# Attention: the fourth head group's causal mask moved from TensorE to GpSimd, and its value product moved behind two more units of row maxima

## What is computed

```python
q, k, v = sh(xn @ Wq.T + bq), sh(xn @ Wk.T + bk), sh(xn @ Wv.T + bv)   # 16 heads of 8
scores = (einsum('bhqd,bhkd->bhqk', q, k) + rel_shift(rel)) * 8 ** (-0.5)
scores = where(mask, NEG, scores)                                      # causal: key after query
p = softmax(scores, axis=-1)
ctx = einsum('bhqk,bhkd->bhqd', p, v)
return ctx @ Wo.T + bo
```

## Time and profile before

| | |
|---|---|
| median of 3 runs | 6254.8 us |
| profiled execution, its own time | 6261.56 us |
| its span | 6259.8 us |
| TensorE busy with matmuls | 5663.6 us (90%) |
| VectorE busy | 4182.8 us (67%) |
| ScalarE busy | 2815.0 us (45%) |
| GpSimd busy | 2135.9 us (34%) |
| exponentials L468 | 640, mean 1451 ns |
| selects L306 and L307 | 480 each, means 645 and 644 ns |
| reductions L362 | 1920, mean 686 ns |

### The profile page before, as it was taken

How to read it: one execution, slowest core, us unless ns; L and a number is a source line. 1 busy time by engine, 2 the same in 40 slices (tenths; PEclk the granted TensorE clock), 3 DMA queues, 4 the chain that set the end, 5 groups by cost and what they waited for, 6 DMA issues and landing times. The chain is left out here.

```text
span 6259.8 us, 121332 instructions
## 1 busy us (share of the span) xinstructions
PE 5663.6 (90%) x38029; PEld 3508.3 (56%) x38029; DVE 4182.8 (67%) x9572; ACT 2815.0 (45%) x4608; POOL 2135.9 (34%) x3000
## 2 busy tenths in 40 slices
PE   7997999999997899879997999889988989886677
PEld 5664444444443677457754776467754556634464
DVE  6875666666665788358854886378835656578764
ACT  4553222222222455535553555445554645533344
POOL 5661000000000666146632665166610012253312
PEclk9998999999998999989998999999998999987799
DMA  4332222222223656046622564066600000000002
GB/s 133 103 106 98 97 96 98 95 96 98 99 94 89 165 155 160 9 121 158 157 63 68 155 160 116 7 165 157 157 13 5 0 7 0 1 4 0 0 2 62
DMA packets 526329, 527.02 MB, mean 84 GB/s; under 512 B 55699, under 2 KB 436706, under 8 KB 503781
## 3 DMA queue, kind: packets, MB, share of 16 engines
q1 hardware_dynamic: 517684, 517.90, 29.7%
q10 hardware_dynamic: 8320, 5.25, 0.4%
HBM read 337.88 MB, written 185.07 MB: 84 GB/s over the span
## 5 line engine op out<-in xcount | busy, mean ns | idle before, releaser
L362 DVE TENSOR_REDUCE a_mx<-a_unit 128x2 f32<-128x512 f32 (+1 forms) x1920 | 1288.2, 686 | 411.8 <-PE a_unit L564 405.5
L468 ACT ACTIVATE a_prob<-a_slot 128x1536 f32<-128x1536 f32 x640 | 928.5, 1451 | 643.3 <-PE a_slot L587 503.4
L562 PE MATMUL a_unit<-a_sk,a_sq 96*128 96x256 bf16 (+3 forms) x5120 | 746.0, 250 | 75.8 <-DMA a_sk<-a_kscratch 41.2
L1177 ACT ACTIVATE f_silu<-f_pG 128x512 f32<-128x512 f32 x528 | 314.8, 598 | 935.0 <-PE f_pG L1252 921.0
L564 PE MATMUL a_unit<-a_maskq,identb 128*128 128x256 bf16 (+1 forms) x1920 | 602.1, 314 | 0.0
L1119 DVE TENSOR_TENSOR f_gated<-f_spread,f_silu 128x512 f32<-128x512 f32 x512 | 354.5, 692 | 351.1 <-ACT f_silu L1177 307.0
L1229 PE MATMUL f_pO<-f_hidden,f_wd 128*128 128x512 f32 x1056 | 545.7, 598 | 13.8 <-DVE f_hidden L1121 13.3
L1252 PE MATMUL f_pG<-f_xnT,f_wg 128*128 128x512 f32 x1056 | 541.1, 594 | 0.0
L1256 PE MATMUL f_pU<-f_xnT,f_wu 128*128 128x512 f32 x1056 | 540.2, 593 | 0.0
L562 PEld LDWEIGHTS a_unit<-a_sk,a_sq 96*128 96x128 bf16 (+1 forms) x5120 | 384.2, 99 | 277.2 <-DVE a_mx L362 154.2
L306 POOL TENSOR_SCALAR_AFFINE_SELECT a_prob<-a_prob 128x512 f32<-128x512 f32 x480 | 309.5, 645 | 578.0 <-ACT a_prob L468 561.4
(11 more groups left out here) (409 smaller groups left out, 11173.0 us busy)
## 6 DMA issues: line engine op xcount, KB each, us to landing
f_spread<-f_scratch SPq DMA_DIRECT2D x1024, 128.0 KB, 2.9
a_sq<-a_qscratch SPq DMA_DIRECT2D x128, 768.0 KB, 5.8
a_sk<-a_kscratch SPq DMA_DIRECT2D x160, 384.0 KB, 6.6
a_qscratch<-a_parts SPq DMA_DIRECT2D x288, 192.0 KB, 2.3
a_qscratch<-a_parts SPq DMA_DIRECT2D x288, 128.0 KB, 2.2
a_kscratch<-a_parts SPq DMA_DIRECT2D x160, 192.0 KB, 2.4
a_kscratch<-a_parts SPq DMA_DIRECT2D x160, 128.0 KB, 2.2
a_qscratch<-a_parts SPq DMA_DIRECT2D x288, 64.0 KB, 1.8
```

The lines of the kernel that those rows point to most:

```text
L362: v.tensor_reduce(dst, src, op=ALU.max, axis=AX.X, negate=True).then_inc(red_done, 1)
L468: act.activation(prob[gr % 2][:, :], slot[:, :], ACT.Exp, scale=SCALE).then_inc(exp_done, 1)
L562: pe.matmul(bank[:, at * wide:(at + 1) * wide], q, sk[b][0:KM, gr * GH + h, 0:wide], start=(at == 0), stop=False)
L1177: act.activation(silu[c % 2][:, :], pG[c % 2][:, :], ACT.Silu).then_inc(silu_done, 1)
```

## The change

GpSimd's `causal` is called for group 3 as well, between the first subtraction and the second BF16 copy of the parts. SELECTED becomes 4, so `scores` writes no mask matmul for any group (L584 and L591 are gone) and `values` waits for the selects in all groups. The value product of group 3, which is done a step late, goes from behind maxima(0) to behind maxima(2). The extra `if` and `sem_inc` around the call only split the block in two.

```diff
@@ -330,6 +330,10 @@
                         pt = parts[j % 2]
                         g.sem_inc(apart, 1)
                         chain.link(g.tensor_tensor(rest[:, :, :], f32s[:, :, :], pt[:, :, 0, :], op=ALU.subtract))
+                    causal(3)
+                    if is_seq(n + 4):
+                        pt = parts[j % 2]
+                        g.sem_inc(apart, 1)
                         chain.link(g.tensor_copy(pt[:, :, 1, :], rest[:, :, :]))
                         g.tensor_tensor(pt[:, :, 2, :], rest[:, :, :], pt[:, :, 1, :], op=ALU.subtract
                                         ).then_inc(parts_done, 1)
@@ -624,9 +628,9 @@
                             ins = pe.transpose(ring[1][:, t * P:(t + 1) * P], xn[:, t, :], ident)
                         ins.then_inc(t_pe, 1)
                     maxima(0)
-                    values(n - 1, (j + 1) % 2, 3)
                     maxima(1)
                     maxima(2)
+                    values(n - 1, (j + 1) % 2, 3)
                     if is_seq(n + 4):
                         if once(n, -4):
                             pe.wait_ge(w_qk, W_QK)
@@ -2637,7 +2641,7 @@
         step(n // 2, n % 2)
 
 
-SELECTED = 3
+SELECTED = 4
```

## The result

| | before | after |
|---|---|---|
| median of the runs | 6258.3 us (4 runs, 6252.84 to 6265.35) | 6362.74 us (4 runs, 6355.85 to 6367.54) |
| profiled execution, its own time | 6261.56 us | 6365.27 us |
| its span | 6259.8 us | 6363.5 us |

The ratio is 1.0165 [1.0148, 1.0183]: 104 us slower, where 44 were forecast, and above the range (6264 to 6330). In the kernel after, lines behind 330 stand 4 further down: L562 is now L566, L580 L584, L587 L591, L610 L614, L635 L639, L362 L366, L468 L472, L333 and L334 L337 and L338. L591 of the kernel after is therefore the unmasked L587 of before, and the masks' own lines (L584 and L591 of before) execute no more.

The account below looks back on a forecast made before the run. TensorE's issue and the waits in front of it were taken to set the step in `attention`. Terms -70.4 + 88.5 + 20.8 + 5 = +44 us on a median of 6254.8 gave 6299 us, range 6264 to 6330.

Parts of the forecast that it names:

- part 1: scores(3) on TensorE, once per sequence: 0.44 us shorter without its masks, 160 times, -70.4 us.
- Part 2: values(n-1, 3) moved: maxima(2) waits 0.61 us for unit 0's reduction, 29 steps in each of five passes, +88.5 us.
- Part 3: maxima(11) waits for reduction 9 behind L67, held by GpSimd's L332: 0.20 us, 26 steps, four `a1` layers, +20.8 us.
- Part 4: GpSimd's selects delay parts, stores and loads before maxima(0): 0.05 us a step in `a1`, +5 us, bounds 0 and +50.
- The cover is not missed: Reduction 0 ends before maxima(2) asks, so moving the value product costs nothing: -50, 6205 us; chance 0.09.
- Part 3 and the loads cost nothing: L67 gets past L332, so reduction 9 is early, and loads add nothing: +18, 6273 us; chance 0.13.
- The loads decide: maxima(0) waits for DMA in each `a1` step: at +0.5 a step +52 more, 6350 us; chance 0.10.
- The clock falls: TensorE idles 0.61 us each step; with one step in ten at 1.2 GHz +240, 6540 us; chance 0.02.

Follow-up runs that it names:

- the freed kernel: The kernel after with the value product at its old place, reduction 9 ahead of L67, stores as each part is ready: 6176.21 us, 0.9864 of before.
- the control: The freed kernel with three groups selected and TensorE's mask kept for the fourth: 6273.88 us, 1.0012 of the kernel before.

## Why the prediction was right and wrong

**The bound and part 1 were right.** scores(3) takes 0.66, and where nothing else is in the way the step is shorter by 0.44 (the freed kernel, and `a0` with the selects alone).

**Part 2 was right**, mechanism and size: 0.61 forecast, 0.60 in the rows, 0.63 a step in the run of the move alone, 88.5 forecast for the whole and +88 measured. Its one omission is the q/k projection, which takes 0.1 more in `a0` and in the written-out steps of `a1`, 3 us in `a0` and some 2 in `a1`.

**Part 3 was right in size** (20.8 forecast, 24 measured) and its place too.

**Part 4 is the term that failed.** "With loads that land sometimes sooner and sometimes later I add 0.05 us a step, 26 x 4 x 0.05 = +5 us" measured +38: 9.4 us in each of four passes, some 0.32 a step. The loop was worked out correctly up to the parts (5.49 against 5.40), and "This loop and TensorE's become equal" had margins of 2.09 and 2.06. What the runs showed in its place:
- The margin was smaller. The 1.35 came from one step and from the median landing. Before the change maxima(0) starts 1.14 us after the landing in the slower of the two rounds, and where it waits for the load it starts 0.12 after it, so 1.02 could be used up.
- The stores land later: 2.51 us after the last issue in the slower round, where it was 2.25. I had taken this as it was. Why they are slower I can't say; with the selects behind L338, where stores are issued 1.3 us sooner, it is 2.28 on average, and with reduction 9 ahead of L67 2.25, though there the step is as long as after the change.
- So the slower round takes 31.68 us for its two steps, and TensorE's own two steps 31.32 (the run with the stores early), where the forecast had some 31.1 for both. The difference of 0.36 is paid as a wait of maxima(0) in every second step. That is not a scatter about equal loops, of which I had counted a half: a step can't be shorter than TensorE's own work, so the faster round doesn't win back what the slower one loses. The bound of +50 that I had put at "1 us later than the median" was the right order.
- Where the load was late by 2 to 3 us, at the end of each `a1` pass, TensorE's clock fell after it. In the kernel after:

```profile
3946.94 0.40 PE L566 MATMUL a_unit<-a_sk,a_sq 96*128 96x128 bf16 x4 [2.15 <-DMA a_sk<-a_kscratch]
...
3948.95 1.10 PE L614 MATMUL a_pctx<-a_prob,a_vaug 128*32 128x256 f32 x8
```

```profile
3946.00:3951.00 5.00, 3.61 (x32) 1.99 (x33) 2.17 (x5) 0.70 (x2) 1.22 (x2) 0.75 0.00 0
```

L614 takes 1.10 instead of 0.66. From maxima(0) to maxima(9) of this layer's last sequence it is 11.40 us, and 10.05 before; the change's own 0.17 leaves 1.2, which I read as the clock. Its wait from maxima(11) to maxima(0) grew too, by 1.4 to 2.7 us in the four layers, so this one step holds some 8 of the 38. The same happened once in the middle of a pass: in the fourth layer maxima(0) waits 1.68 us for a load, at 4285.81, the clock is 0.50 from 4287 to 4292, L639 takes 2.08 us, and maxima(0) to maxima(9) is 2.7 us longer than in the other layers. The prediction gave the ends of the passes no cost of their own.

**The sum.** In the passes -70 + 88 + 24 + 38 = +80, and +98 was measured. By the table the other 18 are 3 in `a0` (7.7 against 29 x 0.17 = 4.9); 10 in maxima(0) to maxima(9) of the `a1` layers (30 against 4 x 4.9), of which the lower clock holds about 5 at the last sequences and 3 in that step of the fourth layer, and the q/k projection some 2; and 5 at the ends of the passes, where 15 masks had been counted as 6.6 us of gain and the ends came out 2 shorter. Outside the passes +6.

**The rivals.** "The cover is not missed" fell with the move alone. "Part 3 and the loads cost nothing" fell. "The loads decide" was half true: maxima(0) did wait for DMA, mostly in every second step and at the ends of the passes, +0.32 a step in place of its 0.5. The time still ended above its 6350, for the 18 and the 6 us that no term of the sum names. "The clock falls" had the right effect at the wrong cause: the waits of 0.46, one in each of some 145 steps, left the clock at 1.00 in every middle stretch; behind five of the six waits of 1.6 us and more for a load, past the first steps of a pass, it fell. By the Trainium skill, TensorE: Matmul & The Clock Gate, Part 1, idling brings the array to half its clock until it is busy again; the trace agrees for waits of 1.68, 2.15 and 2.33 us, and shows none of it for those of 0.46.

## What to carry to other kernels

Before a work item is moved, ask which wait it stands in front of: here 0.81 us of value product between two units hid 0.61 of a reduction's latency, and moving it cost more than the masks gave. When a saving brings a second loop level with the engine's own, cost each of its interleaved rounds by its own landing times and not by the median, and look at what its transfers share; splitting "wait for all, then store all" into stores as each part is ready was worth 46 us with the same bytes. And when an edit for slack shows no gain, try it together with the saving that needed the slack: 64 slower became 85 faster, 64 of it in the passes.

## What was not expected of the hardware

**VectorE held by GpSimd's instructions.** L67's two instructions take 1.85 us when they begin under GpSimd's subtraction L332 (3735.86 to 3737.51) and end 0.34 after it. In the freed kernel they start 0.20 before L332 ends (2962.84 + 1.65 = 2964.49):

```profile
2964.29 0.59 DVE L67 TENSOR_SCALAR a_xn<-h_store,a_moments,a_rstd 128x128 f32 x2
```

0.59 for both, a median of 0.34 each, against 0.93 before; so 0.20 under the end of L332 cost nothing that shows. VectorE's split of the maxima behind reduction 0, 0.17 and 0.19 us before, is longer after the change:

```profile
3725.41 0.64 DVE L400 CAST a_mparts<-a_mx 128x32 bf16<-128x32 f32 x1
3726.13 0.52 DVE L401 TENSOR_TENSOR a_mparts<-a_mx,a_mparts 128x32 bf16<-128x32 f32 x1
```

GpSimd's L338 runs then, later than before:

```profile
3724.38 1.64 POOL L338 TENSOR_TENSOR a_parts<-a_rest,a_parts 128x768 bf16<-128x768 f32 x1
3725.97 0.63 POOL L306 TENSOR_SCALAR_AFFINE_SELECT a_prob<-a_prob 128x512 f32<-128x512 f32 x1
```

L400 ends at 3726.05, 0.03 after L338, and L401 at 3726.65, 0.05 after the select L306. The Trainium skill, SBUF — State Buffer, Who interferes with whom, says that an instruction of VectorE in a mode with two ports and one of GpSimd hold a shared pair of ports in turn and that the second blocks fully; the trace agrees for L67 under L332 and for L400 under L338. The reductions, which read PSUM, kept their 0.69.

**A small write behind large loads.** The 16 KB write took 1.5 us to be usable where it was ahead of the loads and 5.5 where it was 0.4 us behind the first of them (the control).

**A wait of 2 us mostly costs the clock** in a stretch that is otherwise full: 0.75 over 5 us and 0.79 over 8 us in the rows above, and 0.50 over 5 us behind the wait of 1.68. Not each time, though: in the kernel after it stayed at 1.00 behind a wait of 1.74 us (the matmul at 3931.55), and in the kernel with the selects alone behind one of 2.43 (2825.22), where it fell behind the ten others of over 2 us past the first steps of a pass.
